# Angle products of a linear-attention kernel moved from GpSimd to TensorE, and four smaller jobs to ScalarE

## The chip, the core and the metric

The kernel runs on one core of one Trainium2 chip, alone. A core has TensorE (matrix products into PSUM), VectorE, ScalarE, GpSimd and SyncE, each with its own queue of instructions; they meet only at semaphores. The metric is the time of one execution on the device, in microseconds (us): the median of three runs.

## The reference, cut to what matters

One transformer layer over T = 4096 tokens of width 256. The attention part has 8 heads with 64-wide keys and values and 8 "modes" a head; each (mode, head) has its own memory S of 64x64 and its own rotation speed.

```python
angles = pos[:, None, None, None] * omega_scale[None, :, :, None] * inv_freq
qr = l2norm(rotary(q, cos, sin)) * scale      # per mode and head
kr = l2norm(rotary(k, cos, sin))
g = log(clip(sigmoid(x @ Wtg) * rho, 1e-6))
def step(S, inp):
    S = S * exp(b_g)[..., None, None]
    kv = einsum('mbhk,mbhkv->mbhv', k_t, S)
    dv = (v_t[None] - kv) * b_beta[..., None]
    S = S + k_t[..., :, None] * dv[..., None, :]
    o_t = einsum('mbhk,mbhkv->mbhv', q_t, S)
    return S, o_t
o = einsum('tmbhv,hm->bthv', ys, softmax(mode_logits)) * sigmoid(x @ Wg)
x = x + ga * (o @ Wo)
x = x + gb * moe(layernorm(x) * (1 + cb) + sb)   # top 2 of 8 experts, capacity 1024
```

The products of position and speed reach far above one turn, so cosine and sine need the angle in turns, less its whole turns, with more digits than one float32 product has.

## The kernel before, in words

Everything is float32. Three blocks follow each other: attention and routing, the experts, the combination. The change touches only the first, which is most of the time.

It walks over 32 tiles of 128 tokens, and each tile in two halves, `hh` 0 and 1, of 4 heads (8 "quads" `q` of 4 modes x 32 positions or frequencies = 128 partitions). I call the half with `hh == 0` even and the one with `hh == 1` odd; `u` counts halves. The loop body is one odd half and the next even half. The token axis of a tile is cut into `NC` = 4 chunks of `C` = 32 tokens. Inside a chunk the recurrence becomes matrix work with the inverse of a 32x32 triangular system per (mode, head).

Half `u` does two things at once. For the half before it (`v = u - 1`) it runs the four chunks through the memories: `right_sides`, corrections with the inverse, `decayed_corrections`, `update_memories`. For itself it makes angles, rotated keys and queries, decays and the systems, and at the end it inverts all 32 systems in `solve`, a loop of 31 columns with two dependent VectorE instructions each, one operand of which lies in PSUM. Small jobs of the next tile are put between columns through a dictionary `meanwhile` (column number: job). Each engine's queue is written out by hand; the order is that of the calls in its `half`. PSUM banks shared by TensorE and VectorE or ScalarE are passed in turn (`to_dve`, `to_act`).

The steps that matter:

- `angle_parts` (L1087, VectorE) splits the angle of the next half into three short numbers in `tmp` 0 to 2. `low_turns` and `high_turns` (L1455, L1459, GpSimd) multiply each by two entries of the table `turn` and add up: ten instructions over 128x1024. `turns_mod_1`, `add_low_turns`, `turns_end` (L1104 to L1115, VectorE) take off whole turns in the next half, in chunk 0, between the steps of the memories. Then ScalarE makes sine and cosine.
- `squares` (L1476, GpSimd) squares the projected keys and queries in `unit` for their lengths.
- `pw`, the weights of outputs within a chunk, is multiplied by the mode weights `w_quad` on GpSimd (L1496), released by `pw_raw`.
- `expand_te` (L733, ScalarE) copies each chunk's inverses from `tt`, 32 rows a mode, into the block-diagonal tile `te`; `corrections` (L554, TensorE) multiplies `te` with `rhs`, two column sides of 64 a quad, then adds `state` times `qg`.
- `take_dv` (L748, ScalarE) copies the corrections from PSUM. `update_memories` (L1238, VectorE) does `state = state * gc_end + bank_upd` per quad in one fused instruction, then `outT`.
- ScalarE's queue at the end of a half: `v_sb` copies, in even halves the gate, then `front` of the next half (for a new tile: square root of the variance, `hT`, the sigmoids), `roots`, expansions.

```python
for q in range(4 * g, 4 * g + 4):
    sv = state[:, hh * HQ + q].rearrange("p r v -> p (r v)")
    ins = dve.scalar_tensor_tensor(sv, sv, gc_end[:, hh, q, c:c + 1],
                                   bank_upd[g][:, (q % 4) * P:(q % 4) * P + P], ALU.mult, ALU.add)
```

## Time and profile before

| | |
|---|---|
| Median of three runs | 7936.58 us (7935.44 to 7939.62) |
| Profiled execution | 7942.03 us |
| Its span, first to last instruction | 7940.3 us |
| VectorE busy | 6187.8 us, 78% |
| TensorE busy, its mean granted clock | 4718.2 us, 59%; 0.777 |
| ScalarE busy | 3290.2 us, 41% |
| GpSimd busy | 2746.5 us, 35% |
| Even half, odd half in mid run | 116.9 us, 104.4 us |

Busy is time with an instruction at work; the rest of an engine's time it waits or is between instructions. PE is TensorE's products, PEld its loads of the standing operand, DVE VectorE, ACT ScalarE, POOL GpSimd. A granted clock of 1.0 is 2.4 GHz, one of 0.5 is 1.2 GHz. Each float32 product call leaves two records. Lines such as L1078 are lines of the kernel before.

### The profile page before, as it was taken

The page shows a single profiled execution, that of the slowest core. Times are in us where ns is not written, and L with a number is a line of the kernel's source. Part 1 is how long each engine was busy: PE and PEld are TensorE (multiplying, and loading weights), DVE is VectorE, ACT ScalarE, POOL GpSimd, SP SyncE. Part 2 cuts the span into 40 slices and gives each one's busy share as a digit, 9 for nine tenths or more (in the row PEclk, how much of TensorE's full clock was granted, in tenths as well). Part 3 has the DMA queues.
Part 4 walks back from the last instruction along what each step waited for, and adds up shares of the span by engine and source line. Part 5 has one row for each costly group of instructions (what it writes and reads, how often), then busy time and mean ns, then how long its engine had stood idle before and what let it go on. Part 6 is the DMA issues. An engine that isn't in the chain of part 4 may idle for free. (4 is left out here: it accounts for less than half of the span.)

```text
span 7940.3 us, 198838 instructions
## 1 busy us (share of the span) xinstructions
PE 4718.2 (59%) x78633; PEld 4055.4 (51%) x78633; DVE 6187.8 (78%) x12669; ACT 3290.2 (41%) x5527; POOL 2746.5 (35%) x1509
## 2 busy tenths in 40 slices
PE   1566556655566556665566555665566555664994
PEld 0455455555555455555555555555555555554662
DVE  5788888888888888888888888888888888887003
ACT  0444444444444444444444444444444444443220
POOL 1433334333433434333343434333343334432003
PEclk9777777777787777777777777877777777777997
DMA  2000000000000000000000000000000000000223
GB/s 75 1 5 5 5 5 4 5 3 5 5 5 5 5 5 4 5 3 5 5 5 5 5 5 4 5 3 5 5 5 5 5 5 5 4 4 24 80 69 93
DMA packets 60164, 99.98 MB, mean 13 GB/s; under 512 B 11296, under 2 KB 48736, under 8 KB 58080
## 3 DMA queue, kind: packets, MB, share of 16 engines
q1 hardware_dynamic: 50784, 61.66, 2.4%
q0 software_dynamic: 8448, 25.18, 1.1%
q8 instruction: 673, 11.03, 0.6%
q14 instruction: 259, 2.12, 0.1%
HBM read 53.25 MB, written 33.55 MB: 11 GB/s over the span
## 5 line engine op out<-in xcount | busy, mean ns | idle before, releaser
L563 PE MATMUL bank<-rhs,te 128*64 128x64 f32 x8192 | 435.3, 263 | 1137.6 <-DVE rhs L1228 792.8
L563 PEld LDWEIGHTS bank<-rhs,te 128*64 128x64 f32 x8192 | 365.9, 171 | 1217.1 <-DVE rhs L1228 1169.2
L546 PE MATMUL bank<-state,ke 128*64 128x64 f32 x16384 | 708.2, 255 | 268.8 <-DVE outT L1250 155.5
L1488 POOL TENSOR_TENSOR tmp<-raw,cos_t 128x1024 f32<-128x1024 f32 x64 | 151.4, 2366 | 1990.5 <-ACTq L820 1990.5
L546 PEld LDWEIGHTS bank<-state,ke 128*64 128x64 f32 x16384 | 653.4, 167 | 364.9 <-issue 180.2
L582 PE MATMUL last_two<-dvs,kte 128*64 128x64 f32 x16384 | 699.9, 250 | 172.5 <-DVE dvs L1235 172.4
L737 ACT ACTIVATE te<-tt 32x256 f32<-32x256 f32 x1024 | 422.0, 412 | 895.6 <-DVE tt L1212 885.1
L1209 DVE TENSOR_TENSOR last_two<-last_two,prod 128x31 f32<-128x31 f32 (+15 forms) x1984 | 692.5, 349 | 68.1
L582 PEld LDWEIGHTS last_two<-dvs,kte 128*64 128x64 f32 x16384 | 637.5, 163 | 188.8 <-DVE dvs L1235 179.6
L779 ACT ACTIVATE ke<-kq 32x512 f32<-32x512 f32 x1024 | 642.9, 628 | 201.6 <-DVE kq L1161 187.9
L1207 DVE TENSOR_TENSOR prod<-bd,last_two 128x31 f32<-128x31 f32 (+15 forms) x1984 | 671.2, 338 | 68.4
L507 PE MATMUL bank<-kq,ke 128*64 128x64 f32 x16384 | 588.0, 239 | 169.1 <-DVE pw L1194 160.6
L507 PEld LDWEIGHTS bank<-kq,ke 128*64 128x64 f32 x16384 | 566.5, 154 | 177.3 <-DVE pw L1194 102.1
L744 ACT ACTIVATE kte<-kt 32x512 f32<-32x512 f32 x1024 | 641.3, 626 | 27.4 <-PE last_two L582 13.6
L1496 POOL TENSOR_TENSOR pw<-pw,w_quad 128x1024 f32<-128x1024 f32 x64 | 122.3, 1911 | 1518.5 <-DVEq L1359 1518.5
L1450 POOL TENSOR_TENSOR kq<-tmp,turn 128x1024 f32<-128x1024 f32 x320 | 607.2, 1897 | 31.9 <-POOL pw L1496 5.4
L1244 DVE SCALAR_TENSOR_TENSOR state<-state,gc_end,last_two 128x128 f32<-128x128 f32 x2048 | 575.0, 344 | 32.9 <-DVE qg L1186 9.5
L752 ACT ACTIVATE dv<-bank 128x256 f32<-128x256 f32 x512 | 188.0, 379 | 810.3 <-DVE dvs L1235 800.4
L482 PE MATMUL bank<-row_group,select 128*128 128x128 f32 x3072 | 423.2, 292 | 36.2 <-DVE col L1124 27.6
L1225 DVE TENSOR_TENSOR rhs<-bank,eg_col 128x256 f32<-128x256 f32 x512 | 217.4, 425 | 249.5 <-PE bank L546 118.8
L482 PEld LDWEIGHTS bank<-row_group,select 128*128 128x128 f32 x3072 | 380.4, 199 | 54.8 <-DVE col L1124 27.9
L569 PE MATMUL bank<-qg,state 128*64 128x32 f32 x8192 | 405.5, 250 | 0.0
(240 smaller groups left out, 10847.8 us busy)
## 6 DMA issues: line engine op xcount, KB each, us to landing
w_sb<-in_L_ffn_W_dram SPq DMA_DIRECT2D x16, 1024.0 KB, 9.3
expert_rows<-ke SPq DMA_DIRECT2D x1, 8192.0 KB, 21.0
xrows<-expert_rows SPq DMA_DIRECT2D x16, 512.0 KB, 8.5
expert_outputs<-yrow POOLq DMA_DIRECT2D x16, 512.0 KB, 3.4
xt<-_attn_hidden_states_dram SPq DMA_DIRECT2D x32, 128.0 KB, 2.1
xr<-_attn_hidden_states_dram SPq DMA_DIRECT2D x32, 128.0 KB, 2.0
x_after_attention<-xr SPq DMA_DIRECT2D x32, 128.0 KB, 1.7
xo<-x_after_attention SPq DMA_DIRECT2D x32, 128.0 KB
```

Source lines behind the costliest of these rows:

```text
L482: mm = pe.matmul(b[:, ql * P:ql * P + P], select[:, b4 * 4 + ql, :], row_group[:, group, :], start=True, stop=True)
L507: mm = pe.matmul(b[s, q * 2 * C:(q + 1) * 2 * C], ke[:, c, r, q, s], kq[:, r, q, :, c * C:c * C + C], start=(r == 0), stop=(r == 1))
L546: mm = pe.matmul(bank_mem[g][s, q % 4 * DK:q % 4 * DK + DK], ke[:, c, r, q, s], state[:, hh * HQ + q, r, :], start=(r == 0), stop=(r == 1))
L563: pe.matmul(bank_mem[g][s, q % 4 * DK:q % 4 * DK + DK], te[:, q, s], rhs[:, q, :], start=True, stop=True)
L582: mm = pe.matmul(bank_upd[g][s, (q % 4) * P + r * DK:(q % 4) * P + r * DK + DK], kte[:, r, q, s], dvs[:, q, :], start=True, stop=True)
L737: ins = act.activation(te[s, :, 32 * m:32 * m + 32], tt[s, c, :, :], ACT.Copy)
L744: ins = act.activation(kte[s, :, :, 32 * m:32 * m + 32].rearrange("p r q f -> p (r q) f"), kt[s, :, :, c * C:c * C + C].rearrange("p r q f ...
L779: ins = act.activation(ke[s, c, :, :, 32 * m:32 * m + 32].rearrange("p r q j -> p (r q) j"), kq[s, :, :, 0, c * C:c * C + C].rearrange("p ...
L1207: ln(dve.tensor_tensor(pr, a_prob[:, j + 1:C, j:j + 1].broadcast_to([P, rows, cols]), t_prob[:, j:j + 1, 0:cols].broadcast_to([P, rows, co ...
L1209: ln(dve.tensor_tensor(below, below, pr, ALU.subtract))
L1244: ins = dve.scalar_tensor_tensor(sv, sv, gc_end[:, hh, q, c:c + 1], bank_upd[g][:, (q % 4) * P:(q % 4) * P + P], ALU.mult, ALU.add)
L1450: ln(pool.tensor_tensor(low2 if i else into, part, over_t(table), ALU.mult))
```

## The change

It moves work between engines and changes the place of some of it:

1. The products of angle parts and turn tables go to TensorE (`turn_sums`). Once at the start VectorE builds `turn_mat`, a diagonal 32x32 matrix for each table entry and quad. A product multiplies the 32 rows of a mode by its diagonal block; the three parts are added up in PSUM; four modes and four quads fill a bank, low and high tables a bank each. 192 calls a half, issued for the next half, before and after `front`.
2. `turns_mod_1` now reads those banks, in two blocks of four quads, at columns 4 and 20 of `solve` of the half before; nothing of it is left in chunk 0.
3. `corrections` reads `tt` itself with four diagonal 32x32 products a quad in place of two of 128x64; `te` and `expand_te` are gone.
4. `take_dv` on ScalarE first multiplies the memories by `gc_end`, a scaled copy per quad; VectorE's update is one addition for each group of four quads.
5. ScalarE squares the keys and queries straight from PSUM, and scales `pw`, eight copies ahead of `front`.
6. GpSimd keeps the rotation of the queries, `group_rows` and the scatter. `xg` shares the memory of `tmp` 3.

```diff
@@ buffers @@
+        turn_mat = sb("turn_mat", [P, 6, Q, C])
-        te = sb("te", [P, HQ, P])
@@ TensorE @@
             def corrections(v, hh, c):
                 vc = 4 * v + c
                 for g in range(2):
                     pe.wait_ge(sem(f"rhs_ready{g}"), since(f"rhs_ready{g}", vc + 1))
-                    pe.wait_ge(sem("te_ready"), vc + 1)
+                    pe.wait_ge(sem("tt_ready"), v + 1)
+                    pe.sem_inc(sem("pe_held"), 1)
                     for q in range(4 * g, 4 * g + 4):
-                        for s in SIDES:
-                            pe.matmul(bank_mem[g][s, q % 4 * DK:q % 4 * DK + DK], te[:, q, s], rhs[:, q, :], start=True, stop=True)
+                        for s in MODES:
+                            pe.matmul(bank_mem[g][s, q % 4 * DK:q % 4 * DK + DK], tt[s, c, q, :], rhs[s, q, :], start=True, stop=True)
...
+            def turn_sums(u, hh, b4):
+
+                pe.wait_ge(sem("parts_ready"), u + 1)
+                for kind in range(2):
+                    def emit(b):
+                        pe.sem_inc(sem("pe_held"), 1)
+                        for ql in range(4):
+                            q = 4 * b4 + ql
+                            for i, part in enumerate((1, 2, 0)):
+                                for s in MODES:
+                                    mm = pe.matmul(b[s, ql * P:ql * P + P], turn_mat[s, 2 * i + kind, hh * HQ + q, :],
+                                                   tmp[s, part, q * P:q * P + P], start=(i == 0), stop=(i == 2))
+                        return mm
+                    to_dve(emit)
...
                 if not last:
+                    turn_sums(u + 1, 1 - hh, 0)
                     front(*after(n, hh))
                 if hh == 0 and not first:
                     route(n - 1)
                 if not last:
+                    turn_sums(u + 1, 1 - hh, 1)
                     sum_squares(u + 1)
@@ ScalarE @@
+            def take_dv(v, vh, c):
+                act.wait_ge(sem("gc_end_ready"), v + 1)
                 for g in range(2):
+                    act.wait_ge(sem(f"dv_full{g}"), 4 * v + c + 1)
+                    for q in range(4 * g, 4 * g + 4):
+                        ins = act.activation(state[:, vh * HQ + q], state[:, vh * HQ + q], ACT.Copy, scale=gc_end[:, vh, q, c:c + 1])
+                    ins.then_inc(sem(f"state_faded{g}"), 1)
                     act.wait_ge(sem(f"dvs_ready{g}"), since(f"dvs_ready{g}", 4 * v + c + 1))
...
+                act.activation(sq.rearrange("p h t -> p (h t)"), b[:, :], ACT.Square).then_inc(sem("squares_ready"), 1)
                 take(lambda b: act.activation(unit[:].rearrange("p h t -> p (h t)"), b[:, :], ACT.Copy))
...
+                act.wait_ge(sem("pw_raw"), u + 1)
+                for q in range(HQ):
+                    ins = act.activation(pw[:, :, q, :], pw[:, :, q, :], ACT.Copy, scale=w_quad[:, hh * HQ + q:hh * HQ + q + 1])
+                ins.then_inc(sem("pw_ready"), 1)
                 if not last:
-                    front(*after(n, hh))
+                    front(*after(n, hh), v, first)
@@ VectorE @@
+            def turns_mod_1(u, b4):
+
+                s4 = slice(4 * b4, 4 * b4 + 4)
+                whole = prod[:].rearrange("p (q t) -> p q t", q=4)
+                b = full()
+                bv = b[:].rearrange("p (q t) -> p q t", q=4)
+                ln(dve.tensor_scalar(whole, bv, ROUND0, -ROUND0, ALU.add, ALU.add))
+                free(dve.tensor_tensor(sin_t[:, s4], bv, whole, ALU.subtract))
+                b = full()
+                bv = b[:].rearrange("p (q t) -> p q t", q=4)
+                free(dve.tensor_tensor(sin_t[:, s4], bv, sin_t[:, s4], ALU.add))
+                ln(dve.tensor_scalar(whole, sin_t[:, s4], ROUND0, -ROUND0, ALU.add, ALU.add))
+                ins = dve.tensor_tensor(sin_t[:, s4], sin_t[:, s4], whole, ALU.subtract)
...
-                    for q in range(4 * g, 4 * g + 4):
-                        sv = state[:, hh * HQ + q].rearrange("p r v -> p (r v)")
-                        ins = dve.scalar_tensor_tensor(sv, sv, gc_end[:, hh, q, c:c + 1],
-                                                       bank_upd[g][:, (q % 4) * P:(q % 4) * P + P], ALU.mult, ALU.add)
...
+                    dve.wait_ge(sem(f"state_faded{g}"), vc + 1)
+                    sv = state[:, hh * HQ + 4 * g:hh * HQ + 4 * g + 4].rearrange("p q r v -> p (q r v)")
+                    vec(dve.tensor_tensor(sv, bank_upd[g][:, :], sv, ALU.add), f"state_ready{g}", vc + 1)
...
+                if not last:
+                    meanwhile[4] = [lambda: turns_mod_1(u + 1, 0)]
+                    meanwhile[20] = [lambda: turns_mod_1(u + 1, 1)]
@@ GpSimd @@
-            def turns_part(u, hh, first_table, into):
-                for i, part in enumerate((tm[1], tm[2], tm[0])):
-                    table = turn[:, first_table + 2 * i, hh * HQ:hh * HQ + HQ]
-                    ln(pool.tensor_tensor(low2 if i else into, part, over_t(table), ALU.mult))
...
-                vec(pool.tensor_tensor(pw[:], pw[:], w_quad[:, q0:q0 + HQ].unsqueeze(1).unsqueeze(3).broadcast_to([P, NC, HQ, C]), ALU.mult), "pw_ready", u + 1)
-                if not last:
-                    low_turns(*after(n, hh))
-                    squares(u + 1)
-                    high_turns(*after(n, hh))
```

## Rows read from the trace of the kernel before

**Rows 1.** The page: busy us, share of the span and instructions by engine.
```profile
PE 4718.2 (59%) x78633; PEld 4055.4 (51%) x78633; DVE 6187.8 (78%) x12669; ACT 3290.2 (41%) x5527; POOL 2746.5 (35%) x1509
```

**Rows 2.** Even, odd half: length; busy PE, PEld, DVE, ACT, POOL; PEclk.
```profile
3068.99:3185.93 116.94, 66.55 (x1212) 58.53 (x1212) 97.61 (x207) 50.20 (x86) 41.60 (x20) 0.76 0.03 8
3185.93:3290.30 104.37, 67.10 (x1192) 59.05 (x1192) 87.67 (x176) 48.56 (x81) 41.48 (x24) 0.76 0.01 2
```

**Rows 3.** VectorE's waits: who for whom, us in total, times, longest us.
```profile
DVE stat L1065 <- ACT stat L759: 112.3, 32, 3.8
```

**Rows 4.** VectorE beside GpSimd in an inversion (timeline: start us, us, engine).
```profile
3052.45 2.34 POOL L1453 TENSOR_TENSOR tmp<-tmp,kq 128x1024 f32<-128x1024 f32 x1
3052.69 2.66 DVE L1078 TENSOR_TENSOR xg<-gb,cmat 128x512 f32<-128x512 f32 x1
```

**Rows 5.** Five VectorE lines: shortest/median/longest ns, first and last start.
```profile
L1071 DVE COPY gb<-sg x32: 224/1218/1259, 175.4 to 7048.7; 64x128 f32<-64x128 f32 x32
L1078 DVE TENSOR_TENSOR xg<-gb,cmat x32: 693/2657/2665, 180.4 to 7059.6; 128x512 f32<-128x512 f32 x32
L1268 DVE TENSOR_SCALAR xn<-xr,stat x32: 414/1706/1708, 460.9 to 7313.1; 128x256 f32<-128x256 f32 x32
L1278 DVE CAST top_f<-top_i x32: 173/1776/1800, 474.6 to 7317.0; 128x8 f32<-128x8 uint32 x32
L1280 DVE TENSOR_SCALAR chosen<-expert_id,top_f x64: 231/1939/2389, 476.4 to 7317.5; 128x8 f32<-128x8 f32 x64
```

**Rows 6.** Groups by line on VectorE: busy us, mean ns | idle before, releasers.
```profile
L1244 DVE SCALAR_TENSOR_TENSOR state<-state,gc_end,last_two 128x128 f32<-128x128 f32 x2048 | 575.0, 344 | 32.9 <-DVE qg L1186 9.5 <-DVE tmp L1112 5.9 <-PE last_two L582 2.7
L1107 DVE TENSOR_SCALAR cos_t<-tmp 128x1024 f32<-128x1024 f32 x64 | 44.4, 694 | 26.6 <-POOL tmp L1453 21.6
L1115 DVE TENSOR_TENSOR sin_t<-tmp 128x1024 f32<-128x1024 f32 x64 | 78.4, 1224 | 15.3 <-DVE outT L1250 15.2
```

**Rows 7.** VectorE before the loop (timeline): 512 elements from PSUM, then SBUF.
```profile
37.33 0.69 DVE L943 TENSOR_SCALAR tmp<-bank 128x512 f32<-128x512 f32 x1
38.06 0.43 DVE L944 TENSOR_SCALAR tmp<-tmp 128x512 f32<-128x512 f32 x1
```

**Rows 8.** ScalarE around the first norm of an odd half (timeline).
```profile
3032.07 1.28 ACT L759 ACT_TABLE_LOAD   x1 [0.16 <-ACT v_sb L845]
3034.95 0.46 ACT L724 ACTIVATE hT<-bank,mod_col 128x128 f32<-128x128 f32 x1 [1.28 <-PE bank L441]
3035.30 0.77 ACT L726 ACTIVATE hT<-bank,mod_col 128x512 f32<-128x512 f32 x1
3038.84 0.28 ACT L730 ACTIVATE sg<-bank 128x128 f32<-128x128 f32 x1
```

**Rows 9.** TensorE, products of several shapes (timeline).
```profile
3016.91 3.93 PE L507 MATMUL bank<-kq,ke 128*64 128x64 f32 x128
3023.99 3.63 PE L507 MATMUL bank<-kq,ke 128*64 128x64 f32 x64 [3.15 <-DVE pw L1194]
3139.48 2.05 PE L529 MATMUL bank<-hT,wg_sb 128*128 128x128 f32 x16
```

**Rows 10.** VectorE, fifth column of the inversion, even half (timeline).
```profile
3145.50 0.29 DVE L1207 TENSOR_TENSOR prod<-bd,last_two 128x135 f32<-128x135 f32 x1
```

**Rows 11.** Chunk 0, even half; then chunks 0 and 1, odd half (timeline).
```profile
3070.70 1.12 PE L563 MATMUL bank<-rhs,te 128*64 128x64 f32 x16 [9.78 <-ACT te L737]
3189.49 1.01 PE L569 MATMUL bank<-qg,state 128*64 128x32 f32 x16
3190.42 1.54 PE L582 MATMUL last_two<-dvs,kte 128*64 128x64 f32 x32
3199.30 0.69 PE L563 MATMUL bank<-rhs,te 128*64 128x64 f32 x16
3200.79 1.13 ACT L809 ACTIVATE cos_t<-cos_t,half_pi 128x1024 f32<-128x1024 f32 x1
3205.51 0.19 DVE L1250 TENSOR_TENSOR outT<-bank,gateT 128x32 f32<-128x32 f32 x1
```

More of the change, by code:

```diff
@@ L496, in _ @@
             SIDES = (slice(0, 64), slice(64, 128))
+            MODES = tuple(slice(32 * m, 32 * m + 32) for m in range(4))
             def gram(u, c):
@@ L760, in front @@
                     tile_front(n)
+                b = bank_act[turns.bank()]
+                act.wait_ge(sem("act_bank_full"), turns.uses() + 1)
+                if not first:
+                    act.wait_ge(sem("dv_full1"), 4 * v + 4)
+                act.activation(sq.rearrange("p h t -> p (h t)"), b[:, :], ACT.Square).then_inc(sem("squares_ready"), 1)
                 take(lambda b: act.activation(unit[:].rearrange("p h t -> p (h t)"), b[:, :], ACT.Copy))
-                act.sem_inc(sem("raw_ready"), 1)
             def roots(n, hh):
@@ L887, in _ @@
             for c in range(NC):
-                take_dv(v, c)
+                take_dv(v, 1, c)
                 if c < NC - 1:
@@ L1026, in _ @@
             tt2(omega[:], omega[:], er, ALU.mult)
+            for m in range(4):
+                s = slice(32 * m, 32 * m + 32)
+                lp(dve.tensor_tensor(turn_mat[s].rearrange("p i q f -> p (i q) f"),
+                                     turn[s].rearrange("p i q -> p (i q)").unsqueeze(2).broadcast_to([32, 6 * Q, C]),
+                                     ident[s, s].unsqueeze(1).broadcast_to([32, 6 * Q, C]), ALU.mult))
             lp(dve.tensor_copy(pos[:], pos0))
@@ L1493, in half @@
                 vec(pool.tensor_tensor(kq[:, 1, :, 1, :], tm[2], tm[3], ALU.subtract), "q_rotated", u + 1)
[L1495 to L1502 removed]
+                if not last and hh == 1:
+                    group_rows(n + 1)
                 if hh == 0 and not first:
                     scatter(n - 1)
[L1507 removed]
             group_rows(0)
[L1509 to L1510 removed]
             half(0, 0, first=True)
```

100 lines of the change are left out of this document (28 added, 72 removed).

## The prediction

> **What bounds the kernel now.** I read the page first, for the shares. VectorE is busy for 78% of the span, TensorE for 59%, no other engine for half of it [rows 1]. Then the two halves of the loop as stretches. The even half takes 116.9 us, of which VectorE works 97.6; the odd half 104.4, of which it works 87.7; TensorE's granted clock is 0.76 in both [rows 2]. So VectorE's own list of work sets the period of 221.3 us a tile, 31.5 tiles in all counting the ends, and nobody else comes near. Third, the waits of VectorE, to see where another engine sets the pace: once in each odd half it waits for the root of the first norm, 112.3 us in 32 waits, 3.8 at most [rows 3]. Fourth, the timeline beside GpSimd, because some VectorE instructions take far longer than their size. The decay spread starts at 3052.69, while a GpSimd product runs until 3054.79, and takes 2.66 us [rows 4]; the same line took 0.69 once, at 180.4, when GpSimd did nothing large [rows 5]. Instructions of the inversion itself, with one operand in PSUM, show no such stretch. That is the hidden cost of the angle products on GpSimd: not their own time, but VectorE instructions that wait for them.
>
> **What the change removes.** Per tile, in us of VectorE on its path.
> *Waits beside GpSimd.* All eight lines that run beside the angle products and the squares are priced by shortest against median [rows 5]: L1071 0.99, with L1072 and L1077 like it, 3 x 0.99 = 3.0; L1078 1.96; L1268 1.29; L1278 and L1282 like it 2 x 1.60 = 3.2; L1280 twice 1.71 = 3.4. Sum 12.8. The rotation of the queries stays on GpSimd, so the stretches in that stage stay.
> *State updates.* Four fused updates are 4 x 0.281 = 1.12 us (575.0/2048) [rows 6]; one addition of 512 elements from PSUM is 0.69 [rows 7]. That is 0.43 for each of 16 groups a tile. In chunks 2 and 3 VectorE has work of its own between correction and update, which hides what ScalarE and TensorE do; there it counts in full: 8 x 0.43 = 3.4.
> *The rounding in chunk 0.* Two L1107-like and three L1115-like instructions, 2 x 0.69 + 3 x 1.22 = 5.1 us a half [rows 6], leave chunk 0. But they are cover: they stand where VectorE would wait for TensorE. In the odd half the last product for the corrections ends at 3189.49 + 1.01 = 3190.50 and the update products run from 3190.42 for 1.54 [rows 11]; none of this moves. The update can start at 3192.1 and its second group ends at 3194.4; unit_length and the memory read follow, TensorE then has its row products (2.05), and the next corrections start at about 3198.05 where they started at 3199.30 [rows 11]. In chunk 1 the chain passes to ScalarE. Its sines took 4.5, to 3201.92 [rows 11], after the angles were there; now they follow the key expansion of chunk 0 (2.5 from 3193.5) and end at about 3200.4. Then two groups of four fades (1.2, below) and a copy (0.4) end at 3203.6, and the last outT lands at 3204.3 instead of 3205.51. So 1.2 of these 5.1 + 1.7 us is won. In the even half the corrections of chunk 0 start at 3070.70, when te is there [rows 11], 0.75 after their right sides; that wait goes too, and the same walk gives 2.2. Sum 3.4 a tile.
>
> **What it adds.**
> *The rounding in the inversion.* Per block of four quads: four instructions that read PSUM or two SBUF tiles at 0.69, one at 0.43 [rows 5, 7], with 0.18 of gaps: 3.37. Four blocks a tile, nothing to hide behind, since the inversion is VectorE alone: 13.5.
> *The weighing before the root.* ScalarE's queue now holds eight scaled copies behind pw_raw and ahead of the Sqrt of the next tile, its table load and the hT copies. In the odd half VectorE already waits up to 3.8 us for that root [rows 3]; the load starts at 3032.07, straight after the v_sb copies, and starts later by all eight. A scaled copy of 128 elements: 0.28 without pointers, 0.46 with two, so 0.37 with one, and without a wait the next starts 0.11 before the end (3034.95 to 3035.30 is 0.35 for 0.46) [rows 8]. Step about 0.28; eight are 2.3. The ends are 0.25 and 0.46. In the even half gateT and no VectorE wait stand there: nothing.
> The Trainium skill (ScalarE: Activation LUTs, What ACT_TABLE_LOAD costs) gives 186 ns plus 0.833 ns an element, 93 more for a pointer, and 93 of overlap: 0.29 a step, and the term would be 2.3 again; the rows agree for two pointers (0.46).
> *Waiting for the sums.* TensorE gets 192 calls a half, each two records in the trace, of 32x32 by 128. No row has this shape. Nearest below: 64-column products on two sides run 128 records in 3.93, 31 ns each, at full clock, and 64 in 3.63, 57 ns, at half; full-width ones of 128 columns take 2.05/16 = 128 ns [rows 9]. If the four diagonal blocks run side by side, four share about 107 to 128, 27 to 32 ns. I take 30: 2.9 us a bank. The ends are 27 and 128. Odd half: values end at 3031.3, two banks by 3037.1, and VectorE reaches column 4 near 3041: hidden; if the cover were gone it would cost up to 5.8. Even half: the output gate ends at 3141.5 [rows 9], so the banks are full at 3144.4 and 3147.2; VectorE was at column 4 at 3145.50 [rows 10] and, with 1.35 less before it, comes at 3144.15; it waits 0.3 and, 1.4 of work later, 1.3. Term 1.6. The second blocks, at column 20, have 7 us of room. Squares on ScalarE and sum_squares behind the second banks are needed only by unit_length, a whole chunk later.
> *Corrections.* 32 records a group instead of 16; at 30 ns 0.95, about what 16 cost at half clock, 0.45 more at full. Only chunk 3 passes it on, through gram(0): 0.3 a half, 0.6.
> *Once.* turn_mat is four products of 3,072 elements, 1.22 + 2,048 x 1.04 ns = 3.4 each, 13.4 us on the path; against it the first angle sums, for which VectorE waited 21.6 [rows 6], take some 12 less. Zero.
>
> **Sum.** Won 12.8 + 3.4 + 3.4 = 19.6; paid 13.5 + 2.3 + 1.6 + 0.6 = 18.0. Net 1.6 us a tile, x 31.5 = 50. The profiled execution took 7942.0 (span 7940.3), so 7892; the median of the runs lies 5.4 below it: 7886.
>
> **The rivals.**
> *A. The sum stands*, faster by 50. For it: the 12.8 are bare minima against medians, 32 times each.
> *B. ScalarE's fades are late* (the other side). Place: take_dv of chunk 1, right after the sines, and the eight copies before the root. If a scaled copy steps at 0.46, the whole length of the L724 kind, instead of 0.28, the root is 1.4 later and the last outT of chunk 1 1.5 later in both halves, half a us in each chunk 0: 5.4 more a tile, less 1.6, x 31.5 = 120 slower, 8057. It decides from a step of 0.35: 8 x 0.07 before the root and twice 8 x 0.07 in chunk 1 are the 1.6. Against it: the overlap in [rows 8].
> *C. The diagonal blocks don't run side by side.* At 107 ns a record two banks take 20.5: the even half waits 17.8, the odd 10.7, corrections add some 6; 33 a tile, about 8900. At 53 ns, pairs only, 9 a tile, 8170. For it: no row shows two row groups at work; in every product here all 128 rows are one block. The Trainium skill (TensorEngine Tiling (Array Packing), Gotcha 1: PSUM Pressure) says that different row tiles cannot access the same PSUM bank at once, and here all four write one bank, in different partitions; by that rule it is the 8900. No run here shows it so far. Against it: pairs of column blocks into one bank do overlap (31 ns where one alone streams 53 at least) [rows 9].
> *D. TensorE stays at its high clock.* It idles less in the inversion. The products of chunk 0 ran at half clock; at the full one chunk 0 is some 1 to 1.5 shorter in each half: 2.5 a tile, 7807.
>
> **How the numbers follow.** A 0.60, own range 7820 to 7960; B 0.15; C 0.14; D 0.11. The time is A's, 7886. The range takes in D and B's near part and leaves out C: 7770 to 8060. Steps of 0.2% (16 us) are about what a measurement can tell here. Faster: 0.48 of A and D, 0.59; same: 0.08 of A and 0.03 of B, 0.11; slower: 0.04, 0.12 and 0.14, 0.30.
>
> **What would show it.** L1078, L1071 and L1280 at 0.69, 0.22 and 0.23; GpSimd busy about 1000 us. L1065's wait near 6.1 us in odd halves (0.46 a step: 7.5). 192 sum records in 5.8 us, and VectorE's first PSUM read at column 4 waiting 0.3 and 1.3 in even halves only. Chunk 0 with VectorE idle for about 4 us. A period of 219.7. The prediction is wrong if the records come at over 40 ns, or the fades make dv_ready1 the last thing in chunks 0, 2 or 3, or if the loop's longer TensorE program shows waits on issue.

## The result, and the profile after

The changed kernel takes 7960.69 us (median of nine runs, 7951.99 to 7993.16) where the kernel before took 7936.58 beside it: ratio 1.0035, 95% interval 1.0023 to 1.0047. It is slower by 0.35%. I had forecast 7886, faster: the sign is wrong. The profiled execution took 7953.85.

The page of the changed kernel, busy us by engine, and the same two stretches as windows (first the odd half, then the even one; the last three numbers are the granted clock, DMA share and GB/s):

```profile
PE 5413.0 (68%) x111401; PEld 4716.2 (59%) x111401; DVE 5656.2 (71%) x11457; ACT 3642.4 (46%) x7127; POOL 1241.2 (16%) x740
```
```profile
2993.12:3104.95 111.83, 78.12 (x1704) 69.99 (x1704) 83.20 (x160) 55.73 (x110) 18.09 (x12) 0.77 0.01 2
3104.95:3216.20 111.25, 79.91 (x1724) 71.41 (x1724) 87.15 (x188) 54.17 (x107) 16.98 (x7) 0.81 0.02 6
```

Against [rows 1], VectorE works 531.6 us less and TensorE 694.8 more; against [rows 2], the even half is shorter and the odd one longer. So 16.9 us of VectorE's work a tile are gone and no time was won: its idle time grew by 543 us. The question is where it now waits. The view of its waits (who for whom, us in total, times, longest us):

```profile
DVE dvs L1263 <- PE bank L569: 354.6, 260, 1.9
DVE state L1272 <- PE last_two L582: 172.9, 197, 1.4
DVE stat L1090 <- ACT stat L776: 172.8, 32, 6.2
DVE cos_t L1223 <- PE bank L506: 123.3, 63, 4.7
DVE rhs L1253 <- issue: 97.8, 30, 3.5
DVE rhs L1253 <- PE bank L545: 68.0, 68, 1.1
DVE rhs L1256 <- issue: 51.8, 30, 1.9
```

The same view of the kernel before:

```profile
DVE rhs L1225 <- PE bank L546: 118.8, 96, 2.6
DVE dvs L1235 <- PE bank L569: 104.2, 191, 2.1
DVE rhs L1225 <- issue: 99.1, 30, 3.5
DVE cos_t L1193 <- PE bank L507: 90.5, 88, 4.7
```

VectorE waits for the corrections 250 us longer than before, for the updates' products 173 where they hardly showed, for the root 60 longer than in [rows 3], and 51.8 us are marked issue (time in which the engine waited for nothing that the profile shows), 30 times, at a second instruction (L1256) where there was only one such wait before.

To place the loss I cut every half of the middle of the run at the same marks (first right sides; end of the last outT of each chunk; start of the inversion; its end; next half) and took the mean over 29 or 30 halves. "To solve" is from the last outT to the inversion. All in us, worked out from the starts and ends in the traces.

| mean of | chunk 0 | chunk 1 | chunk 2 | chunk 3 | to solve | inversion | to next |
|---|---|---|---|---|---|---|---|
| before, even | 11.04 | 9.74 | 19.57 | 17.14 | 13.56 | 36.91 | 8.13 |
| after, even | 9.72 | 10.09 | 18.10 | 17.26 | 11.72 | 38.09 | 8.08 |
| before, odd | 10.01 | 9.75 | 20.22 | 17.15 | 14.91 | 34.50 | 0.15 |
| after, odd | 11.24 | 9.95 | 18.09 | 17.25 | 16.58 | 36.80 | 0.15 |

A tile is 222.77 before and 223.13 after. The clock granted to TensorE, averaged over the same stages by the windows view: in chunk 0 from 0.69 (even) and 0.73 (odd) to 0.57 and 0.57; in chunk 3 from 0.90 and 0.90 to 0.83 and 0.84; in the inversion, where it hardly matters, from 0.59 and 0.55 up to 0.77 and 0.71.

The timeline of VectorE in chunk 0 of an odd half, changed kernel (start us, us, instruction, in brackets the idle time before it and who ended it):

```profile
2993.12 0.42 DVE L1253 TENSOR_TENSOR rhs<-bank,eg_col 128x256 f32<-128x256 f32 x1 [3.28 <-issue]
2995.18 0.43 DVE L1256 TENSOR_TENSOR rhs<-v_sb,rhs 128x256 f32<-128x256 f32 x1 [1.64 <-issue]
...
2997.96 0.42 DVE L1263 TENSOR_TENSOR dvs<-bank,dec_end 128x256 f32<-128x256 f32 x1 [1.45 <-PE bank L569]
3000.04 0.42 DVE L1263 TENSOR_TENSOR dvs<-bank,dec_end 128x256 f32<-128x256 f32 x1 [1.65 <-PE bank L569]
3001.79 0.69 DVE L1272 TENSOR_TENSOR state<-last_two,state 128x512 f32<-128x512 f32 x1 [1.32 <-PE last_two L582]
```

And TensorE there, and the same corrections two chunks later at full clock (last line):

```profile
2995.84 1.08 PE L563 MATMUL bank<-rhs,tt 32*32 32x64 f32 x32 [13.12 <-DVE rhs L1256]
...
2999.73 1.95 PE L582 MATMUL last_two<-dvs,kte 128*64 128x64 f32 x32
...
3036.08 0.65 PE L563 MATMUL bank<-rhs,tt 32*32 32x64 f32 x32 [1.24 <-DVE rhs L1256]
```

Two things are to be seen. First, 1.64 us of waiting between two instructions of which the second needs nothing but the first. Second, every product of chunk 0 up to the updates takes the time that it has at half clock: 1.08 for the corrections, where two chunks later they take 0.65, and 1.95 for the updates, where [rows 11] has 1.54. VectorE, which had the rounding to do there before, now stands idle at each of them.

Chunk 3 of the same half, TensorE after (`gram(0)`, the products for the systems of chunk 0 of the new half, is the last line):

```profile
3038.57 1.07 PE L563 MATMUL bank<-rhs,tt 32*32 32x64 f32 x32 [1.26 <-DVE rhs L1256]
3039.58 1.07 PE L569 MATMUL bank<-qg,state 128*64 128x32 f32 x16
3040.45 3.66 PE L506 MATMUL bank<-kq,ke 128*64 128x64 f32 x64
```

and two halves of the kernel before (the last line is `gram(0)` of another half than the two above it):

```profile
3007.01 1.12 PE L563 MATMUL bank<-rhs,te 128*64 128x64 f32 x16 [3.35 <-DVE rhs L1228]
3010.42 2.06 PE L507 MATMUL bank<-kq,ke 128*64 128x64 f32 x64
3117.46 3.04 PE L507 MATMUL bank<-kq,ke 128*64 128x64 f32 x64
```

In the first of these halves gram(0) takes 1.6 us less than after the change, full clock against half. That half is the best case: over all halves it took 2.06 to 3.48 before, 2.62 in the mean, and 3.53 in the mean after. VectorE waits for it 2.16 in the half shown. The gap of 1.26 in TensorE's chain is new as well. It comes from here (VectorE after, start us, us):

```profile
3033.03 0.22 DVE L1195 COPY dec_end<-dec 128x32 f32<-128x32 f32 x1 [0.15 <-DVE outT L1274]
3035.46 0.47 DVE L1256 TENSOR_TENSOR rhs<-v_sb,rhs 128x256 f32<-128x256 f32 x1
3036.43 2.00 DVE L1256 TENSOR_TENSOR rhs<-v_sb,rhs 128x256 f32<-128x256 f32 x1
```

The copy, 1.69 before, now falls between two GpSimd products. But the rotation of the queries is still on GpSimd, and a VectorE instruction a little later, with two SBUF inputs, meets its last product and takes 2.00 in place of 0.42.

### The profile page after: what moved, and what is told of

Same layout as the page of the kernel before. It is cut to its first block and busy times, and to the rows that moved or that the text cites. A ratio compares the mean times of both kernels' runs of the same rounds, so it can differ in the third digit from the quotient of the medians.

```text
span 7951.7 us, 264166 instructions
## 1 busy us (share of the span) xinstructions
PE 5413.0 (68%) x111401; PEld 4716.2 (59%) x111401; DVE 5656.2 (71%) x11457; ACT 3642.4 (46%) x7127; POOL 1241.2 (16%) x740
## 5 line engine op out<-in xcount | busy, mean ns | idle before, releaser
L765 ACT ACTIVATE state<-state,gc_end 128x128 f32<-128x128 f32 x2048 | 650.1, 389 | 1432.4 <-PE bank L569 1430.9
L563 PE MATMUL bank<-rhs,tt 32*32 32x64 f32 x16384 | 407.0, 248 | 874.7 <-DVE rhs L1256 874.6
L563 PEld LDWEIGHTS bank<-rhs,tt 32*32 32x32 f32 x16384 | 316.3, 125 | 961.5 <-issue 944.4
L634 PE MATMUL bank<-tmp,turn_mat 32*32 32x128 f32 x24576 | 745.3, 279 | 48.4 <-issue 34.1
L545 PE MATMUL bank<-state,ke 128*64 128x64 f32 x16384 | 647.3, 246 | 167.3 <-issue 128.8
L634 PEld LDWEIGHTS bank<-tmp,turn_mat 32*32 32x32 f32 x24576 | 709.8, 110 | 71.5 <-issue 65.4
L506 PEld LDWEIGHTS bank<-kq,ke 128*64 128x64 f32 x16384 | 617.8, 165 | 129.8 <-DVE pw L1224 77.6
L1272 DVE TENSOR_TENSOR state<-last_two,state 128x512 f32<-128x512 f32 x512 | 354.1, 692 | 205.1 <-PE last_two L582 172.9
L1263 DVE TENSOR_TENSOR dvs<-bank,dec_end 128x256 f32<-128x256 f32 x512 | 217.3, 424 | 363.3 <-PE bank L569 354.6
L1461 POOL DMA_INDIRECT expert_rows<-xn,scatter_at x64 | 64.0, 999 | 2166.1 <-DVE scatter_at L1325 2156.3
```

What stands on the lines that cost most here:

```text
L506: mm = pe.matmul(b[s, q * 2 * C:(q + 1) * 2 * C], ke[:, c, r, q, s], kq[:, r, q, :, c * C:c * C + C], start=(r == 0), stop=(r == 1))
L545: mm = pe.matmul(bank_mem[g][s, q % 4 * DK:q % 4 * DK + DK], ke[:, c, r, q, s], state[:, hh * HQ + q, r, :], start=(r == 0), stop=(r == 1))
L563: pe.matmul(bank_mem[g][s, q % 4 * DK:q % 4 * DK + DK], tt[s, c, q, :], rhs[s, q, :], start=True, stop=True)
L634: mm = pe.matmul(b[s, ql * P:ql * P + P], turn_mat[s, 2 * i + kind, hh * HQ + q, :], tmp[s, part, q * P:q * P + P], start=(i == 0), stop=( ...
L765: ins = act.activation(state[:, vh * HQ + q], state[:, vh * HQ + q], ACT.Copy, scale=gc_end[:, vh, q, c:c + 1])
```

## Experiments

Each ran beside the kernel before, with four to seven executions of its own; the ratio is to that kernel, with its 95% interval. Experiments 1 to 4, 5 to 8 and 9 to 12 ran on the same chip as each other; where a comparison goes beyond that, both the difference of the medians and that of the ratios (x 7,940) are given. Lines such as L1256 shift by a few between kernels; I give the name of the tile.

**1. Eight fills ahead of the loop.**

```diff
+            for _ in range(8):
+                lp(dve.memset(junk[:], 0.0))
             lp(dve.tensor_copy(pos[:], pos0))
```

> The changed kernel with eight fills of a small scratch tile added on VectorE ahead of the loop; nothing inside the loop differs. Theory 1 (placement): the new idle time marked issue at the first instructions of chunk 0 in the odd halves (51.8 us over 30 tiles, about 1.7 us each) is VectorE waiting for instructions that are fetched in blocks of 8,192 bytes, because the head of the loop lies just ahead of the end of a block. Eight more instructions ahead of the loop move its head past that end: the idle time marked issue at the second instruction goes, and the time falls by up to 52 us, to about 7,909. Rival 1: VectorE waits there for other reasons that go with the change (TensorE's longer program, the longer queue of the fades): then eight fills change nothing, and the time stays within 8 us of 7,961.

Measured: 7920.77, ratio 0.9973 (0.9962 to 0.9984): 40 us below the changed kernel by medians, 49 by ratios. The 51.8 us are gone from the waits; the timeline at the loop's head is now

```profile
2958.01 0.42 DVE L1255 TENSOR_TENSOR rhs<-bank,eg_col 128x256 f32<-128x256 f32 x1 [3.46 <-issue]
2958.47 0.43 DVE L1258 TENSOR_TENSOR rhs<-v_sb,rhs 128x256 f32<-128x256 f32 x1
```

That the loop's place costs this is shown, and it alone turned the sign: with the same loop at another address the change is faster by 0.27%. That the cause is the block of 8,192 bytes fits the trace, which has three instruction packets of that size at the loop's head before the fills and two with them, but no run tested it by itself. Even so it is 35 us short of my 7886.

**2. ScalarE's weighing behind the front of the next tile.**

```diff
-                act.wait_ge(sem("pw_raw"), u + 1)
-                for q in range(HQ): ...
-                ins.then_inc(sem("pw_ready"), 1)
                 if not last:
                     front(*after(n, hh), v, first)
+                act.wait_ge(sem("pw_raw"), u + 1)
+                for q in range(HQ): ...
+                ins.then_inc(sem("pw_ready"), 1)
```

> The changed kernel with ScalarE's eight scaled copies of the weights moved behind the exponentials that feed the root's sums; the same work. Theory: in the odd halves VectorE's sums wait about 6.2 us for ScalarE where they waited 3.8 before the change, because the eight copies (2.45 us) stand ahead of them; moved behind, the wait goes back to about 3.8 and the time falls by 2.4 us in each tile, 75 us in all, to about 7,886. Rival: the inversion that follows needs the weights at once, or the wait moves to what comes next: then the fall is below 20 us.

Measured: 7917.81, ratio 0.9968 (0.9956 to 0.9980), 43 (medians) to 53 us below the changed kernel.

```profile
DVE stat L1090 <- ACT stat L776: 116.2, 32, 3.8
DVE rhs L1256 <- issue: 51.6, 30, 1.8
```

The longest wait is back at 3.8 and the sum fell by 56.6, not 75; the wait at issue stands, as it should. The mechanism is right and 57 to 71% of its size reached the end.

**3. The last rounding moved out of the inversion into chunk 0** (with sixteen fills).

```diff
@@ turns_mod_1, at columns 4 and 20 of the inversion @@
-                ln(dve.tensor_scalar(whole, sin_t[:, s4], ROUND0, -ROUND0, ALU.add, ALU.add))
-                ins = dve.tensor_tensor(sin_t[:, s4], sin_t[:, s4], whole, ALU.subtract)
@@ half @@
                 memories(right_sides, 0)
+                ln(dve.tensor_scalar(cos_t[:], sin_t[:], ROUND0, -ROUND0, ALU.add, ALU.add))
+                vec(dve.tensor_tensor(sin_t[:], sin_t[:], cos_t[:], ALU.subtract), "turns_ready", u + 1)
                 memories(decayed_corrections, 0)
```

> The changed kernel with sixteen fills ahead of the loop, and with the last rounding of the angles (one tensor_scalar and one subtraction over all 1,024 columns in place of two and two over 512) moved out of the inversion into chunk 0 of the next half, between the right sides and the corrections. Theory: VectorE is idle for about 4 us in chunk 0, so that work moved there costs little, while the inversion is VectorE's own bound: beside the run with eight fills the time falls by 3 to 5 us in each tile, 95 to 160 us in all. Rival: chunk 0 becomes VectorE's bound as well and the work costs there what it gave back: within 30 us of the run with eight fills.

Measured: 7718.44, ratio 0.9711 (0.9698 to 0.9724), 202 us below experiment 1 (208 by ratios), more than forecast. The inversion is 2.33 and 2.37 us shorter in the two halves; chunk 0, with 1.9 us more of VectorE's work in it, did not grow (9.48 and 9.11 against 10.02 and 9.55). The wait for the corrections fell from 355.0 to 221.8. Chunk 0's idle time in VectorE was real cover, and the change had thrown it away. By the same stages the inversion is 4.7 of the 6.6 us that a tile lost; chunk 0 and chunk 3 each became about a microsecond a tile shorter besides. Why was not tested, nor what sixteen fills do by themselves in place of eight.

**4. The corrections alone**, on the kernel before: `te` and its copies gone, diagonal 32x32 products from `tt`; nothing else.

```diff
-                            pe.matmul(bank_mem[g][s, ...], te[:, q, s], rhs[:, q, :], start=True, stop=True)
+                            pe.matmul(bank_mem[g][s, ...], tt[s, c, q, :], rhs[s, q, :], start=True, stop=True)
```

> The kernel before with one part of the change alone: the corrections of chunks 0 and 1 are taken from the unexpanded inverse by diagonal 32x32 matmuls, and the expanded copy is gone with its ScalarE and TensorE work; angles, fades and weights as before the change. Theory: what ScalarE and TensorE lose in chunk 0 shortens it by 1.2 to 2.2 us in a half while the clock stays as it was: 7,936 less 60 to 107 us. Rival (clock): chunk 0 then stands at half clock throughout as in the changed kernel (0.57 against 0.69 and 0.73), the products at 32 rows do not hold the clock up, and chunk 0 becomes no shorter: within 30 us of 7,936.

Measured: 8036.37, ratio 1.0120 (1.0105 to 1.0136). Slower by 94 us, which neither theory had. Chunk 0 is at clock 0.66 and 0.64, 0.22 shorter in the even half and 0.65 longer in the odd one. Most of the loss is in chunk 3, 17.14 to 18.68 and 17.15 to 18.42, 2.8 us a tile, 89 us in all. Chunk 1 adds 0.44 in each half, at clock 1.00 with and without the change; other stages give some back. TensorE in chunk 3 of a half in which the clock fell early:

```profile
2924.15 0.73 PE L565 MATMUL bank<-rhs,tt 32*32 32x64 f32 x32 [3.44 <-DVE rhs L1215]
2925.81 1.08 PE L565 MATMUL bank<-rhs,tt 32*32 32x64 f32 x32
2927.69 3.66 PE L508 MATMUL bank<-kq,ke 128*64 128x64 f32 x64
```

Over all halves gram(0) went from 2.62 to 3.24 in the mean, and the corrections with the products of `state` and `qg` behind them from 3.13 to 3.73: each is about 0.6 of the 1.4 us by which a half's chunk 3 grew. At full clock, in chunk 1, the new shape costs 0.35 (2.06 to 2.41); the rest is the clock. The kernel before has the same idle time ahead of its corrections (3.35 against 3.44), so the length of the gap alone does not make the difference.

**5. The fades back on VectorE.**

```diff
-                    sv = state[:, hh * HQ + 4 * g:hh * HQ + 4 * g + 4].rearrange("p q r v -> p (q r v)")
-                    vec(dve.tensor_tensor(sv, bank_upd[g][:, :], sv, ALU.add), f"state_ready{g}", vc + 1)
+                    for q in range(4 * g, 4 * g + 4):
+                        ... dve.scalar_tensor_tensor(sv, sv, gc_end[...], bank_upd[g][...], ALU.mult, ALU.add)
```

> The changed kernel with one part undone: the memories fade again in VectorE's own update (four scalar_tensor_tensor of a group in place of one addition over 512 columns) and ScalarE does none of it. Theory (the prediction's term): four take 1.12 us where the one addition takes 0.69, so chunks 2 and 3 become 0.43 us longer for each group, 3.4 us in a tile, and chunks 0 and 1, where VectorE waits for TensorE's updates anyway, somewhat too: 107 to 214 us above the changed kernel, 8,070 to 8,175. Rival: the fades on ScalarE brought nothing, since its copies hold back the rest of its work (rival B of the prediction in a small form): within 30 us of 7,961 or below it.

Measured: 8241.01, ratio 1.0376 (1.0362 to 1.0390), 280 us above the changed kernel (271 by ratios), beyond the top of the forecast. Chunk 2 is 2.5 us longer in each half and chunk 3 1.7, where the fused updates of two groups make 0.86. VectorE's busy time grew by 216 us; its wait for the memory read of the next chunk grew too:

```profile
DVE rhs L1248 <- PE bank L545: 164.7, 68, 2.6
```

That was 68.0: 96.7 us more, 1.5 in each half, which with the 0.86 of work makes up chunk 2. TensorE's clock in chunk 2 is 0.76 and 0.77, from 0.93 and 0.90. A later update makes the memory read later, and this read then runs in a stage with a lower clock. That the one causes the other is argued, not shown. Rival B of the prediction is out: in the changed kernel VectorE waits only 11.4 us in all for ScalarE's fades, and without them the change would be 280 us slower.

**6. The old load put back on GpSimd**, ten operations a half that nothing waits for.

```diff
+                    for k in range(10):
+                        if k % 5 in (0, 1, 3):
+                            ln(pool.tensor_tensor(scratch, select[:], table, ALU.mult))
+                        else:
+                            ln(pool.tensor_tensor(scratch, scratch, select[:], ALU.add))
```

> The changed kernel with ten operations of 128x1024 on GpSimd added in each half during the inversion, as many as the change took away; they write a buffer that nothing reads then. Theory (the prediction's largest term): two-input instructions of VectorE wait beside GpSimd, 12.8 us in a tile as it stood before the change: about 400 us above the changed kernel, 8,360. Rival: the term was too large, because VectorE's waits only move to its next instruction or into idle time: 100 to 200 us.

Measured: 8234.48, ratio 1.0369 (1.0355 to 1.0384), 274 us above the changed kernel (265 by ratios), 8.7 us a tile; between the two expectations, nearer to the rival's. VectorE's busy time grew by 342 us, 10.9 a tile. Two VectorE lines, shortest/median/longest ns:

```profile
L1292 DVE TENSOR_SCALAR xn<-xr,stat x32: 411/1690/1691, 474.9 to 7609.4; 128x256 f32<-128x256 f32 x32
L1104 DVE TENSOR_TENSOR tmp<-gb,cmat x32: 691/691/693, 194.9 to 7354.9; 128x512 f32<-128x512 f32 x32
```

The first is the L1268 of [rows 5], back at its old length, where the changed kernel has 413; the second is L1078, which the load as I placed it does not meet. What it met most is the rounding that the change itself had put into the inversion (busy us, mean ns; changed kernel, then this one):

```profile
L1141 DVE TENSOR_TENSOR sin_t<-sin_t,prod 128x512 f32<-128x512 f32 x128 | 88.6, 692 | 4.4
L1142 DVE TENSOR_TENSOR sin_t<-sin_t,prod 128x512 f32<-128x512 f32 x128 | 202.3, 1580 | 4.4
```

This line and the one before it (427 to 1089 ns) are 198 of the 342 us, and the old kernel had neither of them there. Waits beside GpSimd do cost hundreds of microseconds, but this run does not measure the 12.8 of the prediction: only 143 us, 4.5 a tile, fell on instructions that the old kernel had in this place. The Trainium skill (SBUF — State Buffer, Who interferes with whom) says that VectorE and GpSimd share a pair of ports as an exclusive lock, and that when VectorE is in a mode that takes both ports, which a tensor_scalar can enter, whoever issues second fully blocks; what the trace shows of L1292, a tensor_scalar of 413 ns stretched by 1.3 us, agrees.

**7 and 8. TensorE kept busy ahead of chunk 3, then of chunk 0 too** (on experiment 1).

```diff
+            def hold_clock(count):
+                for _ in range(count):
+                    pe.matmul(bank_upd[0][:, 0:P], select[:, 0, :], ident, start=True, stop=True)
...
+                    hold_clock(20)
                     corrections(v, vh, 3)
```

> The changed kernel with eight fills ahead of the loop (as in the first experiment) and twenty 128x128 matmuls of constants, whose results are overwritten unread, in the 3.3 us in which TensorE waits for the right sides of chunk 3. The run of the corrections alone showed chunk 3 longer by 1.3 to 1.5 us in each half, with TensorE's 64 matmuls of gram(0) at 3.66 us where they took 2.06 before. Theory (clock): the products of 32 rows let the granted clock fall for that stage, and the extra matmuls hold it: gram(0) back near 2.06, chunk 3 shorter by about 1.5 us in each half, some 95 us below the run with the fills alone, about 7,825. Rival: the clock goes by something else in that stage, or VectorE sets its end: within 15 us of 7,921.

Measured: 7878.89, ratio 0.9918 (0.9905 to 0.9932), 42 us below experiment 1 (44 by ratios), half of the forecast. TensorE in chunk 3:

```profile
2872.78 4.73 PE L576 MATMUL last_two<-cmat,select 128*128 128x128 f32 x40
2877.44 0.65 PE L563 MATMUL bank<-rhs,tt 32*32 32x64 f32 x32
2879.68 2.06 PE L506 MATMUL bank<-kq,ke 128*64 128x64 f32 x64
```

gram(0) is at 2.06 in every half and the stage's clock is 1.00: the theory of the clock is shown. Two things ate half of the forecast. Twenty were too many: the corrections of the first group started 2.8 us later behind their right sides than without them, those of the second 1.4. And in the odd half chunk 3 became 1.0 shorter while the stage behind it, where VectorE waits for ScalarE's root, became 1.4 longer: that wait rose from 146.7 to 186.3 us in all.

> The run before, and besides 36 such matmuls from the sixteenth step of the inversion on, ahead of the read of the memories of chunk 0, and in halves that follow the routing 50 more after the inversion. Theory (clock): chunk 0 runs at full clock in place of 0.57: its 32 products of 32 rows in 0.65 us and not 1.08, its updates in 1.13 and not 1.95, and so the waits of VectorE there (some 5.6 us in a half) fall by 2 us: 4 us in a tile, about 125 us below the run before. Rival: TensorE's clock in chunk 0 is not raised by it, or the extra matmuls delay the read: no gain, or a loss up to 60 us.

Measured: 7980.91, ratio 1.0047 (1.0033 to 1.0060), 102 us above experiment 7: a loss, larger than the rival's. A constant product leaves two records. One record follows the other after 0.11 us at full clock (100 in 11.43) and after 0.21 at half, at which the 36 ahead of the read begin (72 records in 10.98). In odd halves the fifty after the inversion ended so late that VectorE waited 7.63 for the corrections:

```profile
2977.93 11.43 PE L576 MATMUL last_two<-cmat,select 128*128 128x128 f32 x100
```

and the 36 ahead of the read made the even half's right sides wait 1.7. The run still says what chunk 0 is worth: at clock 1.00 its even half took 6.58 from the first right sides to the last outT, where it took 9.75; the 1.7 lie ahead of the first right sides and are not in the 6.58.

**9. What helped, together**: experiments 2 and 3 on the changed kernel.

> The changed kernel with the parts that helped put together: sixteen fills ahead of the loop, the last rounding in chunk 0, and the weights' copies behind the exponentials of the root. Theory: the gains add, 7,718 less the 43 us that the order on ScalarE gave: about 7,675. Rival: the waits that the order took away are taken up by something else once the inversion is shorter: within 15 us of 7,718.

Measured: 7666.78, ratio 0.9657 (0.9644 to 0.9670). 52 us below experiment 3 (43 by ratios): the gains add.

**10. And ten constant products ahead of the corrections of chunk 3.**

> The run before with ten matmuls of constants (about 2.3 us at full clock) ahead of the corrections of chunk 3. Theory (clock): twenty of them gave 42 us, though the second half of them stood in the way of the corrections; ten keep the clock as well: 45 to 75 us below the run before. Rival: ten are too few, the 64 matmuls of gram(0) stay at 3.66 us: within 15 us of the run before.

Measured: 7537.27, ratio 0.9493 (0.9480 to 0.9506), 129.5 us below experiment 9, twice the forecast. Chunk 3 is 15.29 in both halves, from 16.79 and 17.33; VectorE's wait for gram(0) is no longer among the nine longest. TensorE:

```profile
2743.09 2.50 PE L576 MATMUL last_two<-cmat,select 128*128 128x128 f32 x20
2745.51 0.65 PE L563 MATMUL bank<-rhs,tt 32*32 32x64 f32 x32
2748.62 2.06 PE L506 MATMUL bank<-kq,ke 128*64 128x64 f32 x64
```

The ten end half a microsecond after the first right sides are there, so the first group's corrections are 0.5 later, and the second group's, which sets the end, are not later at all. It brought three times what experiment 7 did. The traces show two reasons, whose shares were not separated: the corrections are hardly held up, and with experiment 2's order on ScalarE the wait for the root does not grow (83.1 us, from 101.0).

**11. And both clocks.**

> The run before with matmuls of constants for chunk 0 too: 20 (in the half before the routing) or 36 ahead of the read of the memories from step 16 of the inversion on, and 20 more after the inversion where the routing follows. In the earlier run 36 and 36 made the even half's chunk 0 3.2 us shorter (9.75 to 6.58) and, being too long, held the odd one up. Theory: both chunks 0 run at full clock, 6.5 to 7.5 us with the rounding in them, where 9.1 to 9.5 stood: 4 to 5 us in a tile, 125 to 160 us below the run before. Rival: the extra matmuls are still in the way, or the rounding fills the idle time already: within 30 us.

Measured: 7508.50, ratio 0.9455 (0.9442 to 0.9468), 29 us below experiment 10: the rival's figure. The clock in chunk 0 is 1.00, yet chunk 0 only falls from 9.23 to 7.73 (even) and from 9.66 to 9.17 (odd). In the odd half the products are in the way; TensorE there:

```profile
2800.59 0.44 PE L545 MATMUL bank<-state,ke 128*64 128x64 f32 x6 [0.35 <-issue]
2801.35 4.72 PE L576 MATMUL last_two<-cmat,select 128*128 128x128 f32 x40 [0.33 <-issue]
2806.00 0.65 PE L563 MATMUL bank<-rhs,tt 32*32 32x64 f32 x32
```

The right sides of the first group were there at 2802.6. (Experiment 8 had 36 and 50 products in this half, not the 36 and 36 of the expectation.) Fewer products there were not tried. This is the best kernel of the study, 5.4% below the kernel before.

**12. The same products in the kernel before.**

> The kernel before, nothing changed but the same matmuls of constants (20 or 36, and 20 more; ten ahead of the corrections of chunk 3). It tells how much of the last runs' gain has to do with the change. Theory: before the change gram(0) already ran at full clock (2.05 us), so chunk 3 gains nothing; chunk 0 stood at 0.69 and 0.73 and is set in part by ScalarE's expansions, so it gains 1 us or less in a half: 0 to 60 us below 7,940. Rival: chunk 0 is TensorE's there too and gains about 3 us a half: 190 us.

Measured: 7911.05, ratio 0.9961 (0.9947 to 0.9974), 29 us faster: the theory's range, though by another way than I gave. Chunk 3 gained 1.1 us in each half, where I had forecast nothing because I had read gram(0)'s 2.05 from one half; its mean was 2.62. Chunk 0 gained nothing in sum, chunk 2 lost 0.9 and 0.4. So these same products give the kernel before 29 us and gave the best variants 130 and 29. The ten ahead of chunk 3 alone were not run there; the 2.2 us a tile that chunk 3 gained would be some 68 us, an estimate, if nothing else lost by them.

## Why the prediction was wrong

Per tile, predicted against measured, from the table of stages; the last column is experiment 1 cut in the same way, the change without the cost of the loop's place:

| | predicted | measured | with the fills |
|---|---|---|---|
| "to solve", inversion, "to next" | -12.8 + 13.5 + 2.3 + 1.6 = +4.6 | +3.3 | +2.8 |
| chunks 2 and 3 | -3.4 + 0.6 = -2.8 | -3.4 | -2.7 |
| chunks 0 and 1 | -3.4 | +0.5 | -1.0 |
| sum | -1.6 | +0.4 | -0.9 |

**The step that failed** is the walk through chunks 0 and 1, under "the rounding in chunk 0". It says of the products in the odd half that "none of this moves" and starts the update at 3192.1 on that. Two things moved. The loop's head came to a place where VectorE waits for its next instructions, 1.7 us once in a tile: the odd half's chunk 0 and 1 came out 1.43 longer, not 1.2 shorter. Experiment 1 took 40 us off with eight fills outside the loop, enough to turn the sign. The prediction had named waits on issue as a sign of being wrong, but for TensorE's longer program, not for VectorE's.

With the fills the two chunks are still 2.4 us a tile short of the forecast, hidden in the sum because the first row of the table came out 1.8 better. There TensorE's products got slower, not equal. In chunk 0, where the granted clock fell to 0.54 and 0.60 with the fills, the corrections with the products of `state` and `qg` take 4.08 where they took 3.61; in chunk 1, at clock 1.00 in both kernels, 2.41 where they took 2.06. That is 1.6 of the 2.4; the rest was not traced to a term. "Only chunk 3 passes it on", said of the corrections, is part of the same mistake: experiment 4 has chunk 1 0.44 longer in each half.

The clock in chunk 0 is rival D with its sign turned. D said that TensorE, idling less in the inversion, would keep its high clock. The clock did rise there, to 0.77 and 0.71, and fell in chunk 0. D priced the high clock at 1 to 1.5 us in a half; the one half in which experiment 8 held it without late corrections gave 3.2, with right sides 1.7 later.

**A second step was mis-sized: the corrections**, 0.6 a tile in chunk 3 by their record time. Alone they cost 2.8 there and 0.9 in chunk 1 (experiment 4), since the clock is lower for the later corrections and for gram(0) behind them. In the whole change this hid in the good sum of chunks 2 and 3: chunk 3 gained nothing (+0.12 and +0.10), where VectorE's work fell by 0.75 in each half, while chunk 2 gained 1.5 and 2.1.

**The state updates** were sized at 3.4. Taking the fades back costs 280 us, 8.9 a tile (experiment 5). The prediction priced the instruction, not the memory read that starts behind it, for which VectorE then waits 1.5 us longer in each half.

**What held.** The waits beside GpSimd: L1103, the old L1078, takes 0.691 in all 32 places, L1096, the old L1071, 0.22, and L1303, the old L1280, 0.23. VectorE's busy time fell by 16.9 a tile; the terms of the prediction make 12.8 for the waits, 16 x 0.43 = 6.9 for the updates and 2 x 5.1 = 10.2 for the rounding that left chunk 0, less 13.5 for the one that came: 16.4. One such wait was not counted because it did not go but moved: the copy of `dec_end` fell from 1.69 to 0.22, and the group of L1256 has a mean of 624 ns, 100 us more in all than the 429 before. The root: a wait of 6.17 in the odd half shown, predicted 6.1 (the mean of 32 is 5.4, from 3.5), with the eight copies at a step of 0.30:

```profile
3067.35 0.16 DVE L1090 RECIPROCAL stat<-stat 128x1 f32<-128x1 f32 x1 [6.17 <-ACT stat L776]
```
```profile
3063.27 2.45 ACT L872 ACTIVATE pw<-pw,w_quad 128x128 f32<-128x128 f32 x8
3065.73 1.28 ACT L776 ACT_TABLE_LOAD   x1
3067.03 0.29 ACT L776 ACTIVATE stat<-stat,eps_ln 128x1 f32<-128x1 f32 x1
```

GpSimd is busy for 1241 us, where I had said about 1000. The sums: two banks in 5.44 (predicted 5.8), 28 ns a record, so rival C is out:

```profile
3062.45 5.44 PE L634 MATMUL bank<-tmp,turn_mat 32*32 32x128 f32 x192
```

The rule of the Trainium skill (TensorEngine Tiling (Array Packing), Gotcha 1: PSUM Pressure) that different row tiles cannot use one PSUM bank at once would have made this 20 us. Here four diagonal blocks with 32 rows each wrote one bank in their own 32 partitions at 28 ns a record, and the measurement decides. VectorE's waits for the sums were 0.2 and 1.2 us in each even half (6.5 and 36.3 us over 30), predicted 0.3 and 1.3. The rounding in the inversion: two blocks of 3.37 are 6.7 a half, and the inversion grew by 2.30 (odd) and 1.18 (even), since the waits beside GpSimd left it at the same time.

**What stays open.** What the clock of a stage goes by: the runs show that constant products in the wait hold it, and that it is lower in chunk 3 with the 32-row corrections (experiment 4: 0.83 and 0.85 from 0.90), but not whether rows, number or timing of the products decides it. The fall in chunk 0 of the changed kernel has no run of its own: experiment 4 gives 0.66 and 0.64, so the corrections are part of it, and the missing rounding and the new place of the sums were not separated. The table with the fills says in which stages the prediction is short; it does not say why chunks 0 and 1 lack the last 0.8 us a tile. Whether fewer products in the odd half's chunk 0 would give the rest of experiment 11 was not tried.

## What to carry to other kernels

Work taken off the bounding engine is worth something only where nobody else ends the stage: 10.2 us of rounding a tile left chunk 0, a stage of waits, and shortened it by 1.5 (with the fills); moving 1.9 a half back brought 200 us. When products change shape or move, price the stage behind them at both clock levels, and look at the gaps in TensorE's queue ahead of it (1.2 to 3.4 us here); ten constant products in such a gap were worth 130 us; twenty, on another variant, a third of that. Take such a product's time from many halves, not from one: gram(0) had 2.06 in the half that I looked at and 2.62 in the mean. A microsecond won in a stage reaches the end only if no other engine's chain ends the next stage. For differences under 1%, run the loop at a second address before believing the sign.

## What the runs showed of the hardware

- VectorE waited 1.6 to 1.9 us at the second instruction behind the loop's branch, 30 times of 30, on top of the 3.3 at the first; eight instructions more ahead of the loop removed it. The trace has three instruction packets of 8,192 bytes there, at 2990.96, 2993.46 and 2995.84, and that of experiment 1 two, at 2955.94 and 2958.34; over the run the packets of this queue fell from 259 to 229, one in each turn of the loop. That they are VectorE's is inferred from where they stand.
- 32x32 diagonal float32 products took 28 ns a record with 128 columns (192 in 5.44), where a full-width product of 128 columns takes 128 [rows 9]; with 64 columns 20 ns (32 in 0.65), 34 at half clock (32 in 1.08). I read this as four blocks side by side.
- A wait beside GpSimd does not simply go when an instruction is moved or changed: it went to another one with two SBUF inputs (0.42 to 2.00). Two inputs are not needed: beside the load of experiment 6 a tensor_scalar took 1.69 in place of 0.41, a copy 1.29 in place of 0.22, a cast 1.22 in place of 0.17.
- The mean granted clock over a run says little: the change raised it from 0.777 to 0.82 and lowered it in the two stages in which VectorE waits for TensorE.
